# Down of twelve batches with its weights standing and h moving, in a transformer block on one core

## The reference

```python
qkv = relu(einsum('bnc,oc->bno', x, qkv_weight))          # 768 = q, k, v; 32 heads of 8 channels
vk = einsum('bnhe,bnhd->bhed', v_pad, k)                   # v with a column of ones
vk_q = einsum('bhed,bnhd->bnhe', vk, q)
y = einsum('bnc,oc->bno', vk_q[..., :D] / (vk_q[..., D:] + EPS), proj_weight) + proj_bias
x = layernorm(x + y)
h = silu(einsum('bsd,hd->bsh', x, wg)) * einsum('bsd,hd->bsh', x, wu)    # 768 hidden
x = layernorm(x + einsum('bsh,dh->bsd', h, wd))            # wd: 256 x 768
```

## Time and profile before

| | |
|---|---|
| time, median of 3 runs | 493.69 us (493.53 to 493.97) |
| profiled execution, its own time | 493.46 us |
| its span on the core | 491.5 us |
| granted clock of TensorE, mean | 0.999 of full speed |
| PE busy | 485.7 us, 99% of the span |
| VectorE busy | 417.6 us, 85% |
| ScalarE busy | 231.7 us, 47% |
| GpSimd busy | 87.5 us, 18% |
| DMA | 66.42 MB, mean 135 GB/s |

### The profile page before, as it was taken

The page is one execution under the profiler, slowest core; times in us unless marked ns, Lnnn a source line. Parts: engine busy times, 40 slices in busy tenths (PEclk is TensorE's granted clock), DMA queues, the critical chain, the costliest instruction groups (busy, mean ns, idle before and its releaser), DMA issues.

```text
span 491.5 us, 11661 instructions
## 1 busy us (share of the span) xinstructions
PE 485.7 (99%) x4580; PEld 422.9 (86%) x4580; DVE 417.6 (85%) x963; ACT 231.7 (47%) x393; POOL 87.5 (18%) x70
## 2 busy tenths in 40 slices
PE   9999999999999999999999999999999999999996
PEld 5788888888889888898888988888898888989885
DVE  5878878888888888888979888888888888799896
ACT  4667435453453524536254354534535245255553
POOL 1320111311112121111311113111221211113012
PEclk9999999999999999999999999999999999999999
DMA  8325062271614527054270633617145260461212
GB/s 330 144 86 172 2 210 93 90 250 48 226 73 171 171 72 255 15 190 152 85 256 9 232 101 124 217 43 241 58 171 171 76 223 2 173 214 45 87 45 87
DMA packets 49512, 66.42 MB, mean 135 GB/s; under 512 B 3024, under 2 KB 33488, under 8 KB 49488
## 3 DMA queue, kind: packets, MB, share of 16 engines
q1 hardware_dynamic: 49344, 65.82, 38.8%
q10 hardware_dynamic: 144, 0.26, 0.1%
HBM read 35.66 MB, written 23.59 MB: 121 GB/s over the span
## 4 chain that ended last, share of the span: by engine, by line
PE 91%; DVE 6%; POOL 1%; issue 1%; ACT 0%; POOLq 0%; DVEq 0%
PE up_ps L997 33%; PE abcd_ps L997 25%; PE gate_ps L997 25%; PE abcd_ps L1049 4%; PE gate_ps L1027 2%; DVE h L573 1%; PE gate_ps L1168 1%; DVE h_lo L566 1%; DVE st L642 1%; POOL xb L325 1%; DVE r L659 1%; DVE attT_lo L566 0%; DVE att L702 0%; DVE mv L648 0%; ACT h_hi L379 0%
## 5 line engine op out<-in xcount | busy, mean ns | idle before, releaser
L302 POOL TENSOR_TENSOR rstd<-ve,minus_half 128x4 f32<-128x4 f32 (+2 forms) x36 | 43.9, 1219 | 317.0 <-DVE ve L654 316.9
L573 DVE SCALAR_TENSOR_TENSOR h<-up_ps,silu 128x512 f32<-128x512 f32 x95 | 65.3, 688 | 26.5 <-PE up_ps L997 15.5
L379 ACT ACTIVATE h_hi<-h 128x512 fp32r<-128x512 f32 (+1 forms) x97 | 60.6, 626 | 50.0 <-DVE h L573 49.4
L384 ACT ACTIVATE silu<-gate_ps 128x512 f32<-128x512 f32 x95 | 55.8, 587 | 53.6 <-PE gate_ps L997 53.5
L997 PE MATMUL gate_ps<-x1T_lo,wg_hi 128*128 128x512 f32 x192 | 74.9, 390 | 0.0
L997 PE MATMUL gate_ps<-x1T_hi,wg_hi 128*128 128x512 f32 x192 | 74.8, 390 | 0.0
L997 PE MATMUL up_ps<-x1T_hi,wu_hi 128*128 128x512 f32 x192 | 74.8, 389 | 0.0
L997 PE MATMUL up_ps<-x1T_lo,wu_hi 128*128 128x512 f32 x192 | 74.7, 389 | 0.0
L566 DVE TENSOR_TENSOR h_lo<-h,h_hi 128x512 fp32r<-128x512 f32 (+1 forms) x97 | 64.2, 676 | 0.5 <-ACT h_hi L379 0.2
L376 ACT ACTIVATE kv<-abcd_ps 128x512 f32<-128x512 f32 x55 | 32.9, 601 | 65.6 <-PE abcd_ps L997 65.6
L325 POOL TENSOR_TENSOR xb<-x_raw,bias_sb 128x1024 f32<-128x1024 f32 x16 | 38.7, 2421 | 73.2 <-DVE den L596 70.9
(11 more groups left out here) (181 smaller groups left out, 1061.8 us busy)
## 6 DMA issues: line engine op xcount, KB each, us to landing
x_raw<-x_tok SPq DMA_DIRECT2D x16, 512.0 KB, 5.7
att_way<-wg_raw SPq DMA_DIRECT2D x30, 256.0 KB, 2.9
wkv_raw<-att_way SPq DMA_DIRECT2D x30, 256.0 KB, 3.1
xT_raw<-x_chan SPq DMA_DIRECT2D x14, 512.0 KB, 6.1
x_way<-wu_raw SPq DMA_DIRECT2D x28, 256.0 KB, 2.1
wd_raw<-x_way SPq DMA_DIRECT2D x28, 256.0 KB, 3.0
out<-out_sb SPq DMA_DIRECT2D x14, 512.0 KB, 2.7
x<-r SPq DMA_DIRECT2D x13, 512.0 KB, 4.1
```

Of the source, the lines that this page charges most:

```text
L302: nc.gpsimd.tensor_tensor(rs[:, tiles], ve[:, tiles], minus_half[:, tiles], ALU.pow).then_inc(rs_ok, 1)
L379: nc.scalar.activation(dst, src, ACT.Copy).then_inc(ok, 1)
L384: nc.scalar.activation(silu[:, j % 2, :], gate_ps[bank_of(j)][:], ACT.Silu, scale=WSCALE).then_inc(silu_ok[j], 1)
L573: nc.vector.scalar_tensor_tensor(out=h[:, j, :], in0=up_ps[bank_of(j)][:], scalar=WSCALE, in1=silu[:, j % 2, :], op0=ALU.mult, op1=ALU.mul ...
```

## The change

Down of batches 0 to 11 is computed with the weights standing: for each half k of the output's channels and each block j, a 128 x 128 piece of wd_hi stands and 512 tokens of h_hi, then of h_lo, move past it (`down_rows`): 2 x 6 x 2 = 24 matmuls a batch. Blocks 0 to 2 of half 0 come ahead of num, the rest after q. The result has channels in the partitions. VectorE turns its 32 x 32 blocks from PSUM to SBUF (`down_blocks`, in the place of `r2_add`), two DMAs write them to DRAM and two read them back by token, and `r2_back` adds x1, one batch later, between h of blocks 2 and 3 and after attT_lo. By that time r1 holds a later batch, so x1 is kept in DRAM: x1_keep is written from r1 after x1T is back and read into x1 once the r2 of the batch before is done. The output of those batches is normalised by ScalarE (`out_tiles`, in `attention_step`, between the last kv and the first q), with shifts that POOL makes in its loop; POOL takes rstd of x1 ahead of rstd of r2. The factor 1/127 of down is taken into h (`HSCALE`). Some semaphores are merged, and wq_raw and wp_raw become one tile, in whose place the turned-back down lies.

```diff
@@ SP, in the turn
             def turn(i):
-
                 any_i = not isinstance(i, int)
                 if any_i or i + 3 < NB:
                     load_xT(i + 3)
+                if any_i or i >= 2:
+
+                    sp.wait_ge(x1_kept, 16 * (i - 1))
+                    sp.wait_ge(r2_ok[1], i - 1)
+                    sp.dma_start(x1[:].rearrange("p t c -> p (t c)"), x1_keep).then_inc(x1_copied, 16)
                 x1_there_and_back(i)
+
+                sp.wait_ge(x1T_in[KC - 1], 16 * i)
+                if any_i or i < NB - 3:
+                    if any_i or i >= 2:
+                        sp.wait_ge(x1_copied, 16 * (i - 1))
+                    sp.dma_start(x1_keep, r1[:].rearrange("p t c -> p (t c)")).then_inc(x1_kept, 16)
                 if any_i or i >= 2:
                     sp.wait_ge(out_ok, i - 1)
-
-                    sp.wait_ge(x1T_in[KC - 1], 16 * i)
                     sp.dma_start(out[i - 2], out_sb[:].rearrange("p t c -> p (t c)")).then_inc(stored, 16)
-                att_there_and_back(i + 1)
-                sp.wait_ge(r2_ok[1], i)
-                sp.dma_start(x1[:], r1[:]).then_inc(x1_copied, 16)
+                write_blocks(i + 1, att_sq, att_sq_ok, att_way, att_away)
                 sp.wait_ge(xb_ok, i + 2)
                 sp.dma_start(x_raw[:], x[i + 2]).then_inc(x_in, 16)
+                if any_i or i < NB - 3:
+                    down_write(i - 1, 0)
+                read_turned(i + 1, att_way, att_away, attT_raw, attT_in)
+                if any_i or i < NB - 3:
+                    down_write(i - 1, 1)
+                    read_turned(i, down_way, down_away, down_raw, down_in)
...
@@ POOL, in its loop
                 xb_of(i)
+                rstd_1(i)
                 rstd_2(i - 2)
-                rstd_1(i)
+                shift_of(i - 1, mv2, rstd2, rstd2_ok, i - 1)
@@ ScalarE
             def attention_step(i):
+                any_i = not isinstance(i, int)
                 for t in range(NT):
                     kv_relu(t, i + 2, abcd[:, t, :])
+                    if t == 1 and (any_i or i >= 2):
+                        h_hi_of(i - 1, NH - 1)
+                if any_i or i >= 2:
+                    if any_i or i > 2:
+                        act.wait_ge(stored, 16 * (i - 2))
+                    out_tiles(i - 1, out_sb, r2, rstd2, range(NT)).then_inc(out_ok, 1)
                 q_relu(i + 2, q_ps)
                 x1T_hi_spread(i, i)
@@ VectorE
+            def down_blocks(b, k):
+
+                dve.wait_ge(down_mm[k], b + 1)
+                if not isinstance(b, int) or b > 0:
+                    dve.wait_ge(down_away[k], 16 * b)
+                nc.vector.transpose(down_sq[:, k, :].rearrange("p (j t c) -> p t j c", j=NG, t=NT),
+                                    down_ps[k].rearrange("p (t s j) -> p t j s", t=NT, j=NG)).then_inc(down_sq_ok, 1)
+
+            def r2_back(b, k):
+                if isinstance(b, int) and b == 0:
+                    dve.wait_ge(x1_turned_back, 1)
+                else:
+                    dve.wait_ge(x1_copied, 16 * b)
+                dve.wait_ge(down_in[k], 16 * (b + 1))
+                chan = slice(k * P, (k + 1) * P)
+                nc.vector.tensor_tensor(r2[:, :, chan].rearrange("p t (g c) -> p t g c", g=NG), spread(down_raw, k),
+                                        x1[:, :, chan].rearrange("p t (g c) -> p t g c", g=NG), ALU.add).then_inc(r2_ok[k], 1)
+
             def ffn_half(i):
...
             def attention_half(i):
                 r1_of(i)
                 variance_1(i)
-                h_lo_of(i - 1, 4, 5)
+                dve.wait_ge(st2_ok, i - 1)
+                h_of(i - 1, 5)
+                aggregated(st2, mv2, mv2_ok)
+                variance(i - 2, mv2, mv2_ok, ve2, ve2_ok)
                 x1_of(i, r1)
                 x1_blocks(i)
-                out_of(i - 2)
+                h_lo_of(i - 1, 3, 4, 5)
...
@@ VectorE, made_ahead
-                r2_add(i - 1, 0)
-                if not isinstance(i, int) or i + 3 < NB:
-                    xT_lo_of(i + 3)
-                r2_add(i - 1, 1)
+                down_blocks(i - 1, 0)
+                xT_lo_of(i + 3)
+                down_blocks(i - 1, 1)
@@ PE, gate_up of block 1 waits for the banks of down
-                    if late:
+                    if late and turned:
+                        pe.wait_ge(down_sq_ok, 2 * b)
+                    elif late:
                         pe.wait_ge(r2_ok[1], b)
...
+            def down_rows(b, k, blocks, ahead_of_last=None):
+
+                o = slice(k * P, (k + 1) * P)
+                for j in blocks:
+                    if k == 0:
+                        pe.wait_ge(h_lo_ok[j], b + 1)
+                    if j == NH - 1:
+                        with pe.If_ne(flag, 0):
+                            add_up(down_ps[k], [(wd_lo[:, jj, o], part[:, jj, :]) for jj in range(NH)
+                                                for part in (h_hi, h_lo)], start=False, stop=False)
+                    add_up(down_ps[k], [(wd_hi[:, j, o], h_hi[:, j, :])], start=j == 0, stop=False)
+                    if j == blocks[-1] and ahead_of_last:
+                        ahead_of_last()
+                    last = add_up(down_ps[k], [(wd_hi[:, j, o], h_lo[:, j, :])], start=False, stop=j == NH - 1)
+                if NH - 1 in blocks:
+                    last.then_inc(down_mm[k], 1)
@@ PE, attention_half
-                down_of(i - 1, (0,), lambda: num_inputs_beside_kv(i + 1))
+                pe.wait_ge(h_ok[NH - 1], i)
+                down_rows(i - 1, 0, range(NH // 2), lambda: num_inputs_beside_kv(i + 1))
                 num_of(i + 1, q)
                 vk_of(i + 2, vk_ps)
                 q_of(i + 2, q_ps)
-                down_of(i - 1, (1,))
+                down_rows(i - 1, 0, range(NH // 2, NH))
                 pe.wait_ge(q_ok[0], i + 3)
-                down_of(i - 1, (2,))
-                if ahead_of_last_tile:
-                    ahead_of_last_tile()
-                down_of(i - 1, (3,))
+                down_rows(i - 1, 1, range(NH))
```

More of the change, by code:

```diff
@@ L355, in _ @@
             rstd_2(NB - 4)
-            shift_of(1, mv2, rstd2, rstd2_ok, NB - 3)
+            shift_of(NB - 3, mv2, rstd2, rstd2_ok, NB - 3)
             for n in range(2):
@@ L369, in _ @@
                 if n < len(last_tiles) - 1:
-                    shift_of(n + 3, mv2, rstd2, rstd2_part, n + 1, tiles)
+                    shift_of(NB - 1 + n, mv2, rstd2, rstd2_part, n + 1, tiles)
         @block.scalar
@@ L496, in ffn_step @@
                 silu_of(i - 1, 5)
-                h_hi_of(i - 1, 4, 5)
+                h_hi_of(i - 1, 4)
+                if isinstance(i, int) and i == 1:
+                    h_hi_of(i - 1, 5)
             def step(i):
@@ L501, in step @@
                 attention_step(i)
-            def out_tiles(count, dst, src, rs, tiles):
-                act.wait_ge(shift2_ok, count)
-                for t in tiles:
-                    last = nc.scalar.activation(dst[:, t, :], src[:, t, :], ACT.Identity, bias=shift2[:, t:t + 1],
-                                                scale=rs[:, t:t + 1])
-                return last
             def step_before_last(i):
@@ L517, in step_before_last @@
                 act.wait_ge(stored, 16 * (i - 2))
-                out_tiles(1, out_sb, r2, rstd2, range(NT)).then_inc(out_ok, 1)
+                out_tiles(NB - 3, out_sb, r2, rstd2, range(NT)).then_inc(out_ok, 1)
                 x1T_hi_of(2)
@@ L529, in _ @@
             first_step()
-            with act.Fori(2, NB - 3) as i:
+            step(2)
+            with act.Fori(3, NB - 3) as i:
                 step(i)
@@ L541, in _ @@
                 if j < 2:
-                    last = out_tiles(2, att, r2_own, rstd1, (2 + j,))
+                    last = out_tiles(NB - 2, att, r2_own, rstd1, (2 + j,))
                     if j:
@@ L573, in h_of @@
                     nc.vector.scalar_tensor_tensor(
-                        out=h[:, j, :], in0=up_ps[bank_of(j)][:], scalar=WSCALE, in1=silu[:, j % 2, :],
+                        out=h[:, j, :], in0=up_ps[bank_of(j)][:], scalar=HSCALE, in1=silu[:, j % 2, :],
                         op0=ALU.mult, op1=ALU.mult).then_inc(h_ok[j], 1)
@@ L879, in _ @@
             x1T_lo_spread(i)
+            dve.wait_ge(x1_copied, 16 * (i - 1))
             r2_add(i - 1, 0)
@@ L1089, in gate_up @@
                     late = j == 1 and (not isinstance(b, int) or b > 0)
-                    if late:
+                    turned = not isinstance(b, int) or b < NB - 3
+                    if late and turned:
+                        pe.wait_ge(down_sq_ok, 2 * b - 1)
+                    elif late:
                         pe.wait_ge(r2_ok[0], b)
```

130 lines of the change are left out of this document (75 added, 55 removed).

## The result

The changed kernel takes 507.19 us (median of 6 runs, 505.44 to 508.71) against 493.90 (6 runs, 493.53 to 494.10): a ratio of 1.0266, 95% interval 1.0246 to 1.0287. It is slower by 13.3 us, and the time lies above my range. The profiled run took 506.2 us, its span 504.2.

The account below looks back on a forecast made before the run. TensorE was taken to bound the kernel; its 3.66 us gain would be lost to a DMA and VectorE ring: 493.46 - 3.66 + 3.7 = 493.5, with the median 0.23 above: 493.7 us, range 489.6 to 500.5.

Parts of the forecast that it names:

- TensorE's part: Down's matmuls, 48 of 256 columns becoming 24 of 512: saves 0.305 us a batch, 3.66 us for 12 batches.
- VectorE, ScalarE, POOL: Moved work in the loop: VectorE's sum changes by -0.14 us; ScalarE's out tiles, after POOL's rstd2, finish with 2.0 us to spare.
- The ring: Loop of DMAs and VectorE work without PE, from x1 to the next x1T: 29.92 us against PE's 29.495.
- Its part outside the train: VectorE's work from down_in0 to x1's first write, then x1T's return and the next issue: 19.12 us.
- the train: Queue of ten transfers from x1_keep's issue until down_in0 lands, which VectorE awaits in r2_back: taken as 10.8 us.
- A: Time from x1_keep's issue to down_in0's landing: summed to 10.87 us, or 10.58 with a fuller queue, taken as 10.8.
- start and receipt: Fixed cost of the queued transfers up to down_in0, taken from a 0.524 MB store landing after 2.7 us: 1.31 us.
- the traffic: Moving time of three large transfers, four block writes and three block reads up to down_in0: 9.56 us.
- the estimate: From the skill's HBM latency at high load: 1.8 us more for the last transfer, A at 12.6.
- longer ring: Rival: the ten transfers hinder each other, A above about 10.8; at A = 11.4, 500.4 us; chance 0.26.
- 0.54 us late at once: down_in0's first lateness for VectorE's r2_back; each of the ten turns after adds 0.42 us, 4.7 in all.
- a slack of 1.0: Room of h 3 before PE needs it at up of block 5: 1.0 us, cutting 4.7 us lateness to 3.7 lost.

Follow-up runs that it names:

- experiment 1: Kernel before with only TensorE's part of the change (24 matmuls of 512 columns in down), no new DMA or transposes: 490.09 us, ratio 0.9941.
- experiment 8: Changed kernel with x_raw's load after down's reads, and VectorE instead of ScalarE normalising the looped turns' output: 492.70 us, 0.9979 to the kernel before.
- experiment 2: Changed kernel with x_raw's load issued after down's two reads instead of ahead of down's first write: 491.79 us, 0.9964 to the kernel before.
- experiment 3: Changed kernel with x1_keep written twice, a second 0.5 MB store right ahead of the first: 523.86 us, 1.0617 to the kernel before.
- experiment 4: Changed kernel with the first r2_back moved behind attT_lo, next to the second, transfers unchanged: 494.21 us, 1.0013 to the kernel before.
- experiment 7: Changed kernel with the store of out issued after down's two reads, x_raw's load left in place: 494.21 us, 1.0011 to the kernel before.
- experiment 9: Changed kernel with h_lo earlier in the written-out turn, and x1_keep's write, out's store and x_raw's load after down's reads: 489.60 us, 0.9925 to the kernel before.
- experiment 6: Changed kernel with x_raw's load late, h_lo earlier in the written-out turn, and the first r2_back next to the second: 491.48 us, 0.9960 to the kernel before.
- experiment 5: Changed kernel with x_raw's load after down's reads, and h_lo made earlier in the written-out turn: 492.22 us, 0.9965 to the kernel before.

## Why the prediction was wrong

**TensorE's part: right,** and a little under-sized. 0.305 us a turn were forecast; experiment 1 measures 0.36, 4.3 us in all in its turns (3.3 by the medians). The spacing gives 5.76 - 24 x 0.2267 = 0.32 of it; 0.03 more come from gate and up, whose 48 matmuls take 10.88 us there (247.30 to 258.18) and took 10.91. The Trainium skill's spacing (columns over 2.4 GHz plus 2.5 ns, "TensorE: Matmul & The Clock Gate", section "Wait — 56ns, not 53.3ns?") again disagrees: 227 ns for 512 columns, not 216.

**VectorE, ScalarE, POOL: right.** A transpose out of PSUM took 711 ns, with 0.63 us from its start to the next one's (0.65 was taken), and r2_back 689. In the loop PE has no gap before num or q, and experiment 8 shows that ScalarE's new work holds up nobody in a middle turn.

**The ring: right as a mechanism.** VectorE idles before the first r2_back (1.86 us; about 1 was forecast) and not before the second; PE waits before up of block 5 for h; experiments 2, 3 and 4 shorten, lengthen and bypass it, and the turn follows. Its part outside the train was forecast as 19.12 us and is 18.66 (11.72 + 18.66 = 30.38, the turn).

**The step that failed is A,** "I take 10.8, near the row". Over turns 3 to 11 it is 11.72 us (11.40 to 12.07, from SP's timeline to VectorE's). With the shorter rest, the turn comes out 0.46 us over the forecast, 4.1 us in the nine. Of A's two terms, start and receipt were priced as 1.31 us and the traffic as 9.56. The windows show which was mis-sized; changed kernel, the last two columns DMA's share and GB/s:

```profile
283.50:294.00 10.50, 10.50 (x48) 8.71 (x47) 6.60 (x10) 5.25 (x10) 0.00 (x0) 1.00 0.96 324
...
283.50:286.00 2.50, 2.50 (x13) 2.07 (x12) 2.50 (x4) 1.11 (x2) 0.00 (x0) 1.00 1.01 410
...
287.50:289.50 2.00, 2.00 (x10) 1.68 (x9) 0.82 (x2) 1.12 (x3) 0.00 (x0) 1.00 0.84 229
```

The ten transfers move from 283.5 to 294.0: 10.5 us, 0.9 over the 9.56, with 1.3 us in all before and behind them. So the traffic is the term. The block writes start even above's 378, but when x_raw's load and att's first turned read have joined them, the rate falls to 229 GB/s for 2 us. Two stretches of experiment 2, the first of writes, the second with att's turned reads among them, both without the load:

```profile
307.00:309.00 2.00, 2.00 (x11) 1.65 (x10) 1.25 (x2) 0.34 (x1) 0.00 (x0) 1.00 1.02 376
309.50:311.00 1.50, 1.50 (x9) 1.23 (x8) 0.80 (x2) 0.86 (x2) 0.00 (x0) 1.00 0.98 283
```

What 229 GB/s moved in 2 us would have taken 1.2 us at 376 and 1.6 at 283: between 0.4 and 0.8 of the 0.92 by which A was short. But experiment 7 keeps the load in its place and has as short a train as experiment 2, so it isn't the load alone. Why the rate falls, no run tells apart.

Two readings of the train were wrong as well. I took its end for traffic; it is two landings in a row (5.24, then 2.86 us), since SP issues the read only when the write has landed. And I let SP's own issues lie beside the traffic. The block that down's first write carries was ready at 285.09, and the write was issued at 286.37, when SP was through with att's writes and x_raw (VectorE's row, then two of SP's):

```profile
284.38 0.71 DVE L828 STREAM_TRANSPOSE qT_first<-gate_ps 128x512 f32<-128x512 f32 x1
...
283.73 1.79 SPq L225 DMA_DIRECT2D att_way<-wg_raw  x2
285.71 0.54 SPq L271 DMA_DIRECT2D x_raw<-x_tok  x1
```

The two issues of att's writes took SP 1.18 us before, 1.79 here and 0.93 in experiment 9. In experiment 3 the added store shows there alone: down's first write goes out 4.9 us after the first store's issue instead of 3.65, and lands after 5.0 us, as with the change alone. Whether an earlier issue into the same traffic would land earlier was not tried.

The Trainium skill ("DMA: Bandwidth & Descriptors", section "Latency and other measured facts") has HBM's latency growing from 0.2 to 2 us at high load; by it the estimate was 12.6. It pointed to the right side, and the measured excess of 0.92 us is half of its 1.8.

My rival "longer ring" had this mechanism and 500.4 us at A = 11.4, with a chance of 0.26. It was the case that came, and even it was priced too low for the whole kernel, for two reasons that stood in no case of mine:

**The first turns.** "0.54 us late at once", and a slack of 1.0 to cover it, was a steady turn's sum. VectorE's first wait for down_in0 was 2.02 us at once (at 79.28), and turn 1 lost 1.2 us, turn 2 3.45. In turn 2 PE also had a gap before gate of block 0, where the prediction named none:

```profile
102.32 0.47 PE L1050 MATMUL gate_ps<-x1T_hi,wg_hi 128*128 128x512 f32 x1 [1.03 <-DVE x1T_lo L605]
```

The x1T transfers landed late there; the DMA view of 90 to 97 us:

```profile
q8 instruction: 2, 0.03, 2.8%
...
x_way<-wu_raw SPq DMA_DIRECT2D x2, 256.0 KB, 4.0
```

2.2 us is usual. Two loads of instructions, 0.03 MB together, stand beside them. (The loop of VectorE begins at turn 3, not 2, and with the change ScalarE's does too, so turn 2 is written out for both.) In every traced kernel with down's transfers the two loads are there and this pair of writes takes 3.0 to 4.3 us, in experiment 9 too (3.0). So the cause is only seen beside it, not shown. Nor is a ring with slack the whole answer: experiments 4 and 6, where VectorE asks later, still waited 0.78 and 0.55 us for x1T_lo in turn 2. What is seen is that the kernels of experiments 2 and 4 to 8 lose 0.8 to 2.1 us in turn 2, and some scatter (experiment 5: 4.0 us between runs), and that experiment 9 doesn't.

**The written-out turn.** It lost 3.7 us. 1.5 of them are h_lo behind x1's transposes, where down still goes by tiles (experiment 5 against 2). I had worked out that h_lo starts up to 1.8 us later, and asked only who waits in the loop. The other 2.2 weren't taken apart; the ring's wait is among them, 0.89 us before up of block 5.

## What to carry to other kernels

Where a change adds transfers, look for a ring that doesn't pass the bound engine, and sum it round, in queue order, each write that is read back as two landings one after the other. A ring close to the bound's turn leaves no room for an error in the sum: forecast 1.5% over it, it was 3.2% over. The kernels with a ring of 28.8 us, 2% under, still lost in the first turns. Experiment 9's is at most 27.6 by the same sum (18.7, and 8.9 from att's first write to down's first block, which no longer waits for x1T), and it lost nothing there; that its slack is the reason wasn't shown. And put nothing that nobody waits for ahead of the transfer that is awaited: the order of three DMAs, and of h_lo in one turn, is the difference between 507.2 and 489.6 us here.

Follow every moved instruction into the turns that are written out apart; the steady turn doesn't speak for them.

## What the runs showed of the hardware

- Writes to DRAM moved at 410 GB/s; with a load of 0.5 MB and a turned read from DRAM among them it was 229, with turned reads alone 283 (experiment 2). A 256 KB write took 5.24 us to land in that queue, and 2.13 in experiment 9, where only att's two writes were ahead, issued 3.10 us earlier.
- Each half megabyte in the train costs 1.15 to 1.6 us (experiments 3, 7 and 2), against 1.39 by rate alone.
- The issue of two 256 KB writes took SP 0.93 us with no store ahead (experiment 9), 1.79 behind two stores of 0.5 MB, and 2.30 behind three (experiment 3).
- In experiment 3 TensorE waited 3.40, 2.38 and 1.84 us for h, and in or after each of these waits its granted clock was 0.50 for a few us, the lower of its two levels, 1.2 and 2.4 GHz; other waits, of 2.52 us there and of 1.81 us in the changed kernel, left it at 1.00.
- A matmul of 512 columns starts every 0.2267 us, whether x1T or h moves; two of 256 need 0.240.
- VectorE's 32x32 transposes of 128x512 f32 took 706 to 711 ns out of PSUM with a stride of four, and 686 to 690 out of SBUF.
